# Doubled first-head weights at the opening of a four-stage transformer kernel, and the last stage's chunk 0 turned between the last tiles of the second attention

## The reference, cut to what matters

```
x = x + layernorm(attn0(layernorm(x)))      # 16 heads of 64, softmax(q k^T / 8) v, then W_out
x = x + layernorm(moe(layernorm(x)))        # shared expert + top 2 of 8 experts
x = x + layernorm(attn1(layernorm(x)))      # 8 heads, softmax(A1) - lam * softmax(A2), RMS norm, Wo
x = x + layernorm(ffn1(layernorm(x)))       # silu(x w1) * (x w2), gelu(h h1), gelu(h h2), h w3
```

## Time and profile before

| | |
|---|---|
| median of 3 runs | 1955.9 us (1951.54 to 1956.27) |
| the profiled execution | 1958.12 us; its span in the profile 1956.3 us |
| mean granted TensorE clock | 0.977 |
| PE busy | 1821.6 us (93%) |
| PEld busy | 1552.8 us (79%) |
| DVE busy | 1543.6 us (79%) |
| ACT busy | 1365.9 us (70%) |
| POOL busy | 1189.1 us (61%) |

### The profile page before, as it was taken

One profiled execution on the slowest core, in us unless ns is written; L12 is line 12 of the kernel. 1 busy time (PEld: TensorE's weight loads), 2 busy tenths in 40 slices (PEclk: granted clock), 3 DMA queues, 4 the chain that ended last, 5 costly groups with the idle time before them and its releaser, 6 DMA issues.

```text
span 1956.3 us, 36465 instructions
## 1 busy us (share of the span) xinstructions
PE 1821.6 (93%) x11162; PEld 1552.8 (79%) x11162; DVE 1543.6 (79%) x2659; ACT 1365.9 (70%) x2771; POOL 1189.1 (61%) x1480
## 2 busy tenths in 40 slices
PE   4969999999999999987887999999999999999797
PEld 3858888878888888876775788888888888888675
DVE  5958999888989898984367877777777777777675
ACT  3857888787878787842465677777777777777564
POOL 4545656564656565644455867777777777778631
PEclk9989999999999999998998999999999999999898
DMA  2192121221212123112211000000000000100000
GB/s 69 47 91 50 46 48 46 50 47 36 52 44 53 42 51 90 34 60 82 67 58 32 4 1 12 1 11 0 11 0 11 0 11 0 67 1 1 1 1 22
DMA packets 68531, 65.95 MB, mean 34 GB/s; under 512 B 27712, under 2 KB 47040, under 8 KB 68128
## 3 DMA queue, kind: packets, MB, share of 16 engines
q1 hardware_dynamic: 65888, 59.02, 13.6%
q0 software_dynamic: 2496, 5.15, 0.7%
HBM read 21.33 MB, written 9.25 MB: 16 GB/s over the span
## 4 chain that ended last, share of the span: by engine, by line
PE 76%; DVE 8%; issue 5%; ACT 4%; SPq 2%; POOL 2%; DMA 1%; another core or an unknown queue 1%; ACTq 0%; DVEq 0%; POOLq 0%
PE ps_t L633 7%; PE ps_o L643 6%; PE ps_s L665 5%; PE ps_s L666 5%; PE ps_o L644 5%; PE ps_s L1868 5%; PE ps_s L1866 5%; PE ps_s L1867 5%; PE ps_t L1924 3%; PE ps_o L1940 3%; PE ps_o L1942 3%; PE ps_o L1941 3%; DVE a_negmax L2072 2%; PE ps_s L2298 1%; PE ps_s L2299 1%
## 5 line engine op out<-in xcount | busy, mean ns | idle before, releaser
L815 DVE TENSOR_REDUCE a_negmax<-ps_s 128x1 f32<-128x1024 f32 x256 | 313.2, 1224 | 70.8 <-PE ps_s L666 57.4
L2072 DVE TENSOR_REDUCE a_negmax<-ps_s 128x1 f32<-128x1024 f32 x256 | 312.4, 1220 | 64.6 <-PE ps_s L1868 61.6
L746 ACT ACTIVATE a_pth<-ps_t 128x512 fp32r<-128x512 f32 x512 | 279.0, 602 | 115.4 <-PE ps_t L633 115.4
L1998 ACT ACTIVATE a_p<-ps_s,a_negmax 128x1024 f32<-128x1024 f32 x256 | 286.6, 1120 | 96.6 <-DVE a_negmax L2072 95.6
L801 DVE TENSOR_TENSOR a_ptl<-ps_t,a_pth 128x512 fp32r<-128x512 f32 x512 | 327.7, 682 | 6.5 <-ACT a_pth L746 6.2
L881 POOL TENSOR_TENSOR a_rsum<-a_sum,minus_one 128x1 f32<-128x1 f32 x256 | 141.1, 551 | 312.8 <-ACT a_p L776 309.9
L885 POOL TENSOR_SCALAR a_p<-a_p,a_rsum 128x1024 f32<-128x1024 f32 x256 | 289.5, 1131 | 53.4 <-POOL a_rsum L881 53.4
L2169 POOL TENSOR_TENSOR a_p<-a_p 128x1024 f32<-128x1024 f32 x128 | 307.3, 2401 | 10.7
L776 ACT ACTIVATE a_p<-ps_s,a_negmax 128x1024 f32<-128x1024 f32 x256 | 289.0, 1129 | 13.8 <-DVE a_negmax L815 13.8
L665 PE MATMUL ps_s<-a_kh,a_q 128*128 128x512 f32 x512 | 202.9, 396 | 30.2 <-DMA a_kh<-a_kh 26.8
L633 PEld LDWEIGHTS ps_t<-ident_r,a_pr 128*128 128x128 f32 x2048 | 201.1, 140 | 29.8 <-issue 2.6
(11 more groups left out here) (299 smaller groups left out, 4138.1 us busy)
## 6 DMA issues: line engine op xcount, KB each, us to landing
a_q<-a_kh SPq DMA_DIRECT2D x64, 128.0 KB, 2.2
a_q<-a_kl SPq DMA_DIRECT2D x64, 128.0 KB, 2.4
a_kh<-a_kh SPq DMA_DIRECT2D x64, 128.0 KB, 2.2
a_kl<-a_kl SPq DMA_DIRECT2D x64, 128.0 KB, 2.3
a_w_raw<-in_l_w SPq DMA_DIRECT2D x8, 384.0 KB
f_xs_rows<-f_zero SPq DMA_DIRECT2D x4, 736.0 KB, 16.8
f_raw<-in_ffn_w SPq DMA_DIRECT2D x2, 1408.0 KB, 7.4
f_xs<-f_xs_rows SPq DMA_DIRECT2D x2, 1235.0 KB
```

The source lines that it names most:

```text
L815: dve.tensor_reduce(a0_negmax[:, s % 4:s % 4 + 1], ps_s[:, s % 2, :, :], AX.XY, ALU.max, negate=True)\
L2072: dve.tensor_reduce(a1_negmax[:, s % 2, m:m + 1], ps_s[:, m, :, :], AX.XY, ALU.max, negate=True)\
```

## The change

At the opening, the first head's q and k weights are also written twice over side by side (`a0_w1st_hi`, `a0_w1st_lo`, [q q] and [k k]). Sequence 0's q and k of the first head come from these: four pieces (k and q for each 512 tokens) of three products each instead of two pieces. ACT's copy gives both halves of `a0_kh` or of `a0_q`, and DVE's subtraction gives both halves of `a0_kl` or the lower half of `a0_q`. The two placings by DMA (eight DMAs) are gone. Only chunks 0 and 1 are turned before these products; chunk 2 is turned after them, and chunk 3 in slots 0 to 3 of the first head, on each engine. SP issues x chunks 0 and 1 first, then the q/k weights, x chunks 2 and 3, and the value weights. POOL keeps only the router's clears ahead of its first `norm_rstd`; the router's other constants follow chunk 3's factors, ahead of the first division.

At the end, chunk 0's second norm is applied in slot 18 (`DRAIN`) and chunk 1's in slot 19, each with its POOL factor in the same slot; chunk 0 is turned in slot 19 behind the last weighing. The projections of slots 17, 18 and 20 go to `ps_m`, that of 19 to one bank of `ps_s`, that of 21 to `ps_o`, with waits for the additions that free `ps_m`. ACT does a one-column Silu in slot 18. The last stage starts with two pairs of products of chunk 0, turns chunk 1, and goes on; its bank order over `ps_s` is turned round.

```diff
+        a0_w1st_hi = named.enter_context(nc.sbuf_tensor("a0_w1st_hi", [P, 2, 2 * DH0], F32R))
+        a0_w1st_lo = named.enter_context(nc.sbuf_tensor("a0_w1st_lo", [P, 2, 2 * DH0], F32R))
...
         def input_dve(dve):
...
+            x_stats(dve, 0)
+            x_stats(dve, 1)
+            for c in range(2):
+                x_norm(dve, c)
+            x_lo(dve, 0)
+            x_stats(dve, 2)
+            x_lo(dve, 1)
...
         def input_pool(pool):
...
-            f0_pool_const(pool)
-            for c in range(NC):
+            f0_pool_clear(pool)
+            for c in range(2):
                 norm_rstd(pool, NORM_IN + c, c)
 
         def input_sp(sp):
...
-                if c == 0:
-                    a0_load_first(sp)
+                if c == 1:
+                    sp.dma_start(a0_wqk_raw[:, :], t["l0_wqk"][0]).then_inc(S["a0_wqk_loaded"], 16)
+            a0_load_wv(sp, 0)
...
+        def a0_pe_first(pe, i):
+            half, kind = A0_FIRST[i]
+            w_hi, w_lo = (a[:, "qk".index(kind), :] for a in (a0_w1st_hi, a0_w1st_lo))
+            x = slice(half * BANK, (half + 1) * BANK)
+            pe.matmul(first_bank(i), w_hi, xT_hi[:, x], start=True, stop=False)
+            pe.matmul(first_bank(i), w_hi, xT_lo[:, x], start=False, stop=False)
+            pe.matmul(first_bank(i), w_lo, xT_hi[:, x], start=False, stop=True).then_inc(S["a0_split_in"], 1)
...
+        def a0_act_first(act, i):
+            half, kind = A0_FIRST[i]
+            dst = a0_q if kind == "q" else a0_kh
+            act.wait_ge(S["a0_split_in"], i + 1)
+            act.activation(dst[0][:, half * BANK:(half + 1) * BANK], first_bank(i), ACT.Copy).then_inc(S["a0_split_hi"], 1)
...
         def a0_pe(pe):
-            pe.wait_ge(S["x_lo"], NC)
-            pe.wait_ge(S["a0_w_lo"], 1)
-            for i, s in enumerate(A0_NEXT):
-                a0_pe_split(pe, A0_PIECES[0][s], first_bank(i))
+            pe.wait_ge(S["a0_w1st_lo"], 1)
+            for i in range(len(A0_FIRST)):
+                if i % 2 == 0:
+                    pe.wait_ge(S["x_lo"], i // 2 + 1)
+                a0_pe_first(pe, i)
+            input_pe_turn(pe, 2)
...
-                    if s in (0, KT):
-                        pe.wait_ge(S["a0_kh_copied"], 64 * h + (32 if s == 0 else 64))
-                        pe.wait_ge(S["a0_kl_copied"], 64 * h + (32 if s == 0 else 64))
+                    if first and s == 0:
+                        pe.wait_ge(S["a0_split_lo"], len(A0_FIRST))
+                    elif s in (0, KT):
+                        pe.wait_ge(S["a0_kh_copied"], 64 * h + (0 if s == 0 else 32))
+                        pe.wait_ge(S["a0_kl_copied"], 64 * h + (0 if s == 0 else 32))
...
+                    if first and s == 2:
+                        input_pe_turn(pe, 3)
+                    if first and s in (1, 3):
+                        pe.wait_ge(S["x_lo"], 3 if s == 1 else NC)
+                        pe.wait_ge(S["a0_w_lo"], 1)
...
+                    if first and s == 2:
+                        turn_act(act, TURN_IN + 3, 3)
...
         def a0_dve(dve):
-            for i, s in enumerate(A0_NEXT):
-                a0_dve_split(dve, i + 1, A0_PIECES[0][s], first_bank(i))
+            for i in range(len(A0_FIRST)):
+                a0_dve_first(dve, i)
+                if i == 1:
+                    x_norm(dve, 2)
+            x_lo(dve, 2)
...
+                    if first and s == 0:
+                        x_stats(dve, 3)
+                    elif first and s == 1:
+                        x_norm(dve, 3)
+                    elif first and s == 3:
+                        x_lo(dve, 3)
...
+            pool.tensor_scalar(twice(a0_w1st_hi), w, 1.0, 0.0, ALU.mult, ALU.add).then_inc(S["a0_w1st_hi"], 1)
+            pool.wait_ge(S["a0_w1st_hi"], 1)
+            pool.tensor_tensor(twice(a0_w1st_lo), w, twice(a0_w1st_hi), ALU.subtract).then_inc(S["a0_w1st_lo"], 1)
             weights(0)
+            norm_rstd(pool, NORM_IN + 2, 2)
             value_weights(0)
+            norm_rstd(pool, NORM_IN + 3, 3)
+            f0_pool_const(pool)
...
         def a0_sp(sp):
-            for i, s in enumerate(A0_NEXT):
-                a0_place_qk(sp, i, i + 1, A0_PIECES[0][s])
             f0_load_small(sp)
...
-        A1_NORM_PAIR = (SLOTS - 2, SLOTS - 1, SLOTS, SLOTS + 1, SLOTS + 4)
-        A1_RSTD = (SLOTS - 2, SLOTS + 3)
+        A1_NORM_PAIR = (SLOTS - 2, SLOTS - 1, SLOTS, SLOTS + 1)
+        A1_RSTD = SLOTS - 2
+        DRAIN = SLOTS + 2
...
-            if s > SLOTS:
-                return ps_s[:, s % 4 // 2, s % 2, :]
+            if s == DRAIN + 1:
+                return ps_s[:, 0, 0, :]
+            if s == DRAIN + 3:
+                return ps_o[:, :]
             return ps_m[:, :]
...
-                if s <= SLOTS:
+                if s <= DRAIN:
                     pe.wait_ge(S["a1_added"], from0(g))
-                elif s == SLOTS + 1:
+                elif s == DRAIN + 1:
                     pe.wait_ge(S["a1_exped"], 2 * H1 * SLOTS)
+                elif s == DRAIN + 2:
+                    pe.wait_ge(S["a1_added"], g - 1)
...
                 if a1_lag(s, LAG_PV, first):
                     weigh(h, s)
+                if s == DRAIN + 1:
+                    f1_pe_turn(pe, 0)
...
+                if s == DRAIN:
+                    act.activation(a1_lexp[:, 0, 0:1], minus_one[:, :], ACT.Silu)
+                if s == DRAIN + 1:
+                    turn_act(act, TURN_A1, 0)
...
+                if s == DRAIN + 1:
+                    turn_dve(dve, TURN_A1, 0, ps_t[:, 0, :])
+                if s in (DRAIN, DRAIN + 1):
+                    i = s - DRAIN
+                    norm_apply(dve, NORM_A1 + 2 + i, i, lambda k: tile(X, i * TPC + k), lambda k: tile(xst[i], k))\
+                        .then_inc(S["xst_ready"], 1)
...
+                if s in (DRAIN, DRAIN + 1):
+                    norm_rstd(pool, NORM_A1 + 2 + s - DRAIN, s - DRAIN)
...
         def f1_bank(use):
-            return ps_s[:, use % 4 // 2, use % 2, :]
+            return ps_s[:, 1 - use % 4 // 2, use % 2, :]
...
+            pe.wait_ge(S["a1_added"], H1 * SLOTS - 2)
...
-            for i in range(2):
-                first_layer(0, i)
+            first_layer(0, 0, range(2))
+            f1_pe_turn(pe, 1)
+            first_layer(0, 0, range(2, HT))
+            first_layer(0, 1)
...
             for j in range(2 * HT):
+                if j == 2:
+                    turn_act(act, TURN_A1 + 1, 1)
                 silu(0, j)
...
+                    if p == 0 and j == 1:
+                        turn_dve(dve, TURN_A1 + 1, 1, ps_t[:, 1, :])
```

More of the change, by code:

```diff
@@ L122, in sandwich_kernel @@
         a0_pth = [sb(f"a0_pth{i}", [P, KT, BANK], F32R) for i in range(2)]
-        a0_ptl = [sb(f"a0_ptl{i}", [P, KT, BANK], F32R) for i in range(2)]
+        a0_ptl = [sb("a0_ptl0", [P, KT, BANK], F32R)]
+        named = ExitStack()
+        a0_w1st_hi = named.enter_context(nc.sbuf_tensor("a0_w1st_hi", [P, 2, 2 * DH0], F32R))
+        a0_w1st_lo = named.enter_context(nc.sbuf_tensor("a0_w1st_lo", [P, 2, 2 * DH0], F32R))
+        named.close()
+        a0_ptl.append(sb("a0_ptl1", [P, KT, BANK], F32R))
         a0_o = [sb(f"a0_o{i}", [P, BANK]) for i in range(4)]
@@ L490, in input_dve, with x_stats, x_norm, x_lo @@
             dve.memset(Y[:, :, :], 0.0).then_inc(S["y_zero"], 1)
[L492 to L507, removed]
+            x_stats(dve, 0)
+            x_stats(dve, 1)
+            for c in range(2):
+                x_norm(dve, c)
+            x_lo(dve, 0)
+            x_stats(dve, 2)
+            x_lo(dve, 1)
+        def x_stats(dve, c):
+            dve.wait_ge(S["x_loaded"][c], 16)
+            norm_stats(dve, NORM_IN + c, c, lambda i: tile(X, c * TPC + i))
+        def x_norm(dve, c):
+            dve.wait_ge(S["x_turned"], from0(c - 1))
+            norm_apply(dve, NORM_IN + c, c, lambda i: tile(X, c * TPC + i), lambda i: tile(xst[c % 2], i))\
+                .then_inc(S["xst_ready"], 1)
+        def x_lo(dve, c):
+            turn_dve(dve, TURN_IN + c, c, ps_t[:, c % 2, :])
         def input_pool(pool):
@@ L557, in sandwich_kernel @@
         A0_QUAD_SPLITS = sum(len(z) for z in A0_SPLITS)
+        A0_FIRST = [(half, kind) for half in range(2) for kind in ("k", "q")]
         def a0_pair(p, j):
@@ L572, in a0_splits @@
             n = sum(1 for z in A0_SPLITS[j] if z <= s and not (last and j == QUAD - 1 and z in A0_NEXT))
-            return p * A0_QUAD_SPLITS + (len(A0_NEXT) + sum(len(z) for z in A0_SPLITS[:j]) + n)
+            return p * A0_QUAD_SPLITS + (len(A0_FIRST) + sum(len(z) for z in A0_SPLITS[:j]) + n)
         def a0_outs(p, j, s):
@@ L1153, in f0_pe_prefix, with f0_pool_clear @@
             pe.matmul(bank, ones[:, :], f0_sum[0][:, g, 4:, :], start=False, stop=True).then_inc(S["f0_prefix"], 1)
+        def f0_pool_clear(pool):
+            pool.memset(f0_zero[:, :], 0.0)
+            pool.memset(f0_taken[:, :, :, :], 0.0)
+            for i in range(2):
```

(11 more changed lines are left out.)

70 lines of the change are left out of this document (40 added, 30 removed).

## The result

On the chip the changed kernel takes 1937.8 us (median of 4 runs, 1935.85 to 1940.53) against 1956.1 us (1951.54 to 1956.9) for the kernel before: a ratio of 0.9912, 95% interval 0.9893 to 0.9932, or 18.3 us less. The forecast was 1937.6, or 18.3 us less. The profiled execution took 1935.85 us, its span is 1932.5.

The account below looks back on a forecast made before the run. PE is busy 93% of the span, so only the two seams can win: 12.4 us at the opening plus 5.9 at the end, 18.3 from the 1955.9 median, gives 1937.6 us; range 1931 to 1944.

Parts of the forecast that it names:

- First score product at 17.6: Opening: doubled products from 10.65 us replace the DMA placings; first score product at 17.6 instead of 33.29, 15.7 us earlier.
- 3.3 us given back until slot 3's projection, and then nothing: Head 0, slots 0 to 3: moved chunk work cuts the 15.7 us lead to 12.4 at slot 3's projection, which then stays.
- POOL's constants cost nothing: First slots: factor 3 and constants precede the first division; tile 0 at 29.8, wanted at 30.9, costed at nothing.
- rival 2: First slots: POOL's constants run longer beside DVE, tile 0 comes 3 us late, total 1940.6 us; chance 0.10.
- The clearing stall slides: After head 1's slot 3: PE's 16.4 us wait for SP's router clearing keeps its length and comes about 12.4 us earlier.
- rival 3: Clearing stall: a queue sets its end, so it takes the opening's gain, leaving 5.9 us, total 1950.0; chance 0.08.
- The end, 5.9 us: Last stage: first gate 6.5 us earlier, chunk 1's low part gives back 0.6, net 5.9; bounds 4.0 to 6.5.
- rival 1: End: Square needs its own table, so table loads return around slot 19; 2 us lost, total 1939.6; chance 0.12.
- Rivals 4 and 5: 4: PE stays at lower clock through first head, 1985 us, chance 0.03. 5: moved chunk work hidden, 1934.3, chance 0.05.
- early table load bring silu 0 forward: Last stage: silu 0 at 1849.5, since the table load of 1.28 us was done in slot 18.
- 2 to 3 us between chips: Whole kernel: chip-to-chip spread of the forecast time, beside 2 us from the estimates of handovers.

Follow-up runs that it names:

- doubling by itself: The kernel before with only the first head's products made from doubled weights, all four chunks still turned first: 1943.3 us in one run.
- idle products: The changed kernel plus 24 products nobody reads on PE in slots 2 and 3 of head 0: 1914.3 us, ratio 0.9904 to the kernel before.
- chunk 3 moved forward: The changed kernel with chunk 3's statistics, norm, copy and low part earlier, POOL's constants ahead of its factor: 1911.5 us, ratio 0.9886; again 1934.8 us, 0.9897.
- The end alone: The kernel before with only the edits at the second attention's end and the last stage: 1928.0 us, ratio 0.9972.
- first experiments: Four runs on one chip (opening's edits only, end's edits only, idle products, chunk 3 moved forward), where the kernel before takes 1934.4 us.
- deferral alone: The kernel before with chunks 2 and 3 moved behind the first products, constants and loads reordered, q and k still placed by DMA: 1952.8 us in one run.

## Why the prediction was right, and the term that was off

- *First score product at 17.6.* It came at 17.82, behind DVE's low part of q and no DMA. The doubled products started at 10.90 (forecast 10.65), one every 0.43 us, at the lower level as expected. Right. And doubling by itself costs the slots nothing (its lead is 7.9 us at slot 0 and 8.4 at slot 8).
- *3.3 us given back until slot 3's projection, and then nothing.* This is the mis-sized term. By the rows, the first score product leads by 33.29 - 17.82 = 15.5 us (forecast 15.7), slot 3's projection by 42.06 - 30.38 = 11.7 (forecast 12.4; the earlier trace rows), and slot 8's mark by 10.35. So 3.8 us went back until the projection instead of 3.3, near enough to the working; but another 1.3 us went behind it, where I had written that the old order holds and the 12.4 us stay. There the projection's three products and slot 4's four score products ran at 0.63 us and more. With idle products the projection is at 30.07, a lead of 12.0, and slot 8's mark still leads by 12.0: the step was right in its mechanism, and TensorE's lower level took the rest. In the changed kernel's second profile, with the projection at the higher level, only 0.3 us went behind it. I had priced the lower level only as a rival for a whole head, and thought the changed kernel safe from it after the start; it came back at 26 us, behind PE's wait of 2.25 us, and idle products in the waits keep it away. That the 3.8 us were not necessary either is what chunk 3 moved forward shows: projection at 28.21, lead 13.9, kept to slot 8.
- *POOL's constants cost nothing, rival 2.* Tile 0 was ready at 29.25 (forecast 29.8) and wanted at 31.83: right as a wait of PE. But they lay beside DVE's apply, which took 1.62 us instead of 1.11, a cost on another engine that I hadn't counted. What it added to the giving back can't be told apart from the rest.
- *The clearing stall slides, rival 3.* It slid, and rival 3 is out: PE's wait is 15.3 us against 16.4, and SP began 11.6 us earlier (86.08 against 97.69). That the stretch is 1.05 us shorter can't be put down to the change.
- *The end, 5.9 us.* The gate is 7.1 us nearer to the last mark (forecast 6.5), and the whole tail 6.51 us shorter, just at my upper bound of 6.5. The end alone gives 5.4 us by the ratio, 6.4 by the medians and 6.7 in its profile, so 5.9 lies among what was measured. The order of events is as forecast, and so are the 0.6 us that went back in the first layer, where chunk 1's low part (0.68 us at 1835.15) now stands. One piece of the reasoning earned nothing: I let the early table load bring silu 0 forward, and the gate comes at the same time without it.
- *Square needs its own table, rival 1.* False: the Square at 1825.39 follows the Silu without a load. The Trainium skill, "ScalarE: Activation LUTs", section "Table sets: the hidden batching unit", names relu, copy, identity and abs as what every set has; here Square runs behind a Silu without a load as well. The 2.66 us that the Trainium skill gives for a switch with its drain (same page, section "What ACT_TABLE_LOAD costs") aren't seen either: where the load stands in front of the first silu, ACT ends the last Square at 1835.76, and the silu starts at 1837.17, 1.4 us later.
- *Rivals 4 and 5.* The lower level did come back, but for ten microseconds and not for a head; the moved work was far from hidden.
- *The absolute time.* I had put 2 to 3 us between chips. The kernel before took 1934.4 us on the chip of the first experiments and 1955.5 on that of the last, 21 us apart. That 1937.6 was met therefore says less than the ratio, 0.991 beside both of the changed kernel's groups of runs.

The sum came out right in part by luck: 2.0 us less from the opening (10.35 for 12.4) met 1.7 us more from the stall and the end and 0.8 from the slots of both attentions, and of these 2.5 us only the 0.6 of the end lie where the change acts.

## What to carry to other kernels

A step moved from an empty opening into the first slots of a loop can cost more than its instructions: each handover it adds is a wait in a row with the loop's own, and the lower clock level can come back among PE's waits. Here the doubling, which moves nothing, kept its lead whole, and the deferral lost half of its own. Put such steps in the order in which their results are wanted on every engine, not only on one. And price a long wait that the change leaves in place: splitting one burst of DMAs that stood ahead of a small, urgent one was worth nearly as much as the whole change (16.8 us against 17.4 on the same chip).

## What the runs showed of the hardware

TensorE's granted clock fell to 0.50 between 26 and 36 us, after five microseconds in which PE was busy for 1.81 us, and did not when PE was kept busy in them. Where it falls differs between two executions of one code: in the second it fell near 18 us, behind waits of 0.78 and 0.79 us, and stayed up through a wait of 2.24 us that ended at 25.69. So the length of one wait doesn't tell. The record of the clock isn't the whole story either: it stands at 1.00 from 10 to 15 us of the changed kernel, where products of 512 columns take 0.63 us, one every 0.43, as they do where it stands at 0.50.

DVE's apply of a chunk, four subtract-and-scales, took 1.11 us with POOL idle or at a factor, and 1.54, 1.62, 1.67 and 1.93 us beside memsets, the constants or a division on POOL. With deferral alone it took 1.21 beside the same memsets. What in POOL's work causes this was not tried.

The expert stage took 201.1 and 205.4 us in two executions of the changed kernel, 199.7 to 206.2 us in nine of the thirteen profiles and 183 to 185 us in the other four, all from the first experiments' chip. Why is open; it moved the spans of single profiles by half of what the opening gained, and only marks taken before it tell the opening's worth.
